# Four chained convolution layers: the second convolution's five shifted products become one, on columns skewed by row

## The reference: what is computed

```
x = x + newton_schulz_inverse(_gn(x), 5 iterations)          # layer 0, one 128x128 matrix per channel
x = x + quantised_conv3x3(_gn(x), weight_int8, scale, bias)   # layer 1
x = x + conv5x5(_gn(x), filter_w[..., :, None] * eye(5))      # layer 2
x = x + circular_conv3x3(_gn(x), weight)                      # layer 3, written with FFTs
```

## Time and profile before

| | |
|---|---|
| three runs | 4611.87, 4616.66, 4623.76 us |
| profiled execution, its own time | 4624.59 us |
| its span | 4622.8 us |
| first stage | up to about 2562 us |
| second stage | the rest, to 4622.8 us |
| TensorE matmul busy | 4399.1 us, 95% of the span |
| VectorE, ScalarE, GpSimd busy | 83%, 49%, 56% |
| mean granted TensorE clock | 0.986 |

### The profile page before, as it was taken

How to read it: one execution, slowest core, us unless ns; L and a number is a source line. 1 busy time by engine, 2 the same in 40 slices (tenths; PEclk the granted TensorE clock), 3 DMA queues, 4 the chain that set the end, 5 groups by cost and what they waited for, 6 DMA issues and landing times. The chain is left out here.

```text
span 4622.8 us, 79863 instructions
## 1 busy us (share of the span) xinstructions
PE 4399.1 (95%) x24265; PEld 3045.4 (66%) x24265; DVE 3833.0 (83%) x8224; ACT 2251.8 (49%) x4551; POOL 2610.2 (56%) x2957
## 2 busy tenths in 40 slices
PE   7999999999999999999999599999999999999998
PEld 6888888888888888888888244444444444444443
DVE  7988898889888988988896687787787778778774
ACT  4766776777677766777776122222222222222221
POOL 7888888888888888888887122222222222222221
PEclk9999999999999999999999799999999999999999
DMA  1111111111111111211111365555556555555554
GB/s 59 61 48 56 56 56 56 56 56 56 56 56 56 56 56 47 63 49 56 56 56 37 84 137 130 130 134 137 125 132 139 127 130 136 132 128 134 137 127 85
DMA packets 333591, 403.08 MB, mean 87 GB/s; under 512 B 23088, under 2 KB 286032, under 8 KB 316880
## 3 DMA queue, kind: packets, MB, share of 16 engines
q1 hardware_dynamic: 284112, 269.46, 18.2%
q10 hardware_dynamic: 49152, 129.59, 16.8%
HBM read 135.22 MB, written 134.22 MB: 58 GB/s over the span
## 5 line engine op out<-in xcount | busy, mean ns | idle before, releaser
L288 POOL TENSOR_TENSOR M<-two,YX 128x256 f32<-128x256 f32 x2560 | 1827.0, 741 | 402.6 <-ACT YX L363 373.4
L758 PE MATMUL bank<-YX,M 128*128 128x256 f32 x8192 | 1948.5, 386 | 40.1 <-issue 40.1
L1147 PE MATMUL bank<-xn,wt 128*128 128x512 f16 (+1 forms) x6912 | 1660.2, 381 | 25.6 <-DVE xn L1003 17.9
L758 PEld LDWEIGHTS bank<-YX,M 128*128 128x128 f32 x8192 | 1504.1, 192 | 227.3 <-issue 44.5
L363 ACT ACTIVATE YX<-bank 128x512 f32<-128x512 f32 x2048 | 1227.5, 599 | 690.8 <-PE bank L758 684.8
L920 POOL TENSOR_TENSOR xn<-F,xn 128x2048 f16<-128x2048 f32 x128 | 487.8, 3811 | 1577.6 <-ACT xn L957 1577.6
L1147 PEld LDWEIGHTS bank<-xn,wt 128*128 128x128 f16 (+1 forms) x6912 | 672.9, 100 | 810.5 <-issue 18.8
L1021 DVE SCALAR_TENSOR_TENSOR x<-bank,wu,x 128x512 f32<-128x512 f32 x512 | 382.2, 746 | 294.7 <-PE bank L1154 283.8
L1154 PE MATMUL bank<-xh,wth 96*128 96x512 f16 (+1 forms) x1792 | 515.4, 380 | 15.3 <-DMA xh<-xn 15.3
L957 ACT ACTIVATE xn<-F 128x2048 f16<-128x2048 f32 x128 | 244.7, 1912 | 475.1 <-DVE F L1077 475.1
L410 DVE BATCH_NORM_STATS2 st<-X 128x6 f32<-128x256 f32 x1024 | 367.8, 410 | 9.6 <-DMA X<-in_x 9.6
(11 more groups left out here) (107 smaller groups left out, 3580.6 us busy)
## 6 DMA issues: line engine op xcount, KB each, us to landing
xh<-xn ACTq DMA_DIRECT2D x768, 131.8 KB, 4.3
X<-in_x SPq DMA_DIRECT2D x64, 1024.0 KB, 4.8
x_scratch<-X SPq DMA_DIRECT2D x64, 1024.0 KB, 5.7
x<-x_scratch SPq DMA_DIRECT2D x64, 1024.0 KB, 6.1
out<-x SPq DMA_DIRECT2D x64, 1024.0 KB, 3.8
xh<-xn ACTq DMA_DIRECT2D x384, 65.9 KB, 2.4
wf<-in_w SPq DMA_DIRECT2D x2, 192.0 KB, 8.5
wf<-in_w SPq DMA_DIRECT2D x1, 320.0 KB, 8.5
```

The costliest lines, as they stand in the source:

```text
L288: nc.gpsimd.tensor_tensor(M[odd][:, at, :], two[:, :].unsqueeze(1).broadcast_to([H, 2, H]), YX[odd][:, at, 0:H], ALU.subtract).then_inc(ma ...
L758: ins = nc.tensor.matmul(banks[u % A_RING][:, 2 * H * m:2 * H * (m + 1)], M[odd][:, 2 * p + m, :], YX[odd][:, 2 * p + m, :], start=True, s ...
L1147: nc.tensor.matmul(bank, wt[l][:, a, k, :], v, start=(k == a == b == 0), stop=False)
```

## The change

The diagonal filter is put on the diagonal of the data. Eight DMAs for an image copy the two f16 halves (`xn2`, now one tile for all images) to a skewed tile `xd`, in which row r of a block lies r columns further left. An output and the five inputs that it reads then stand in the same column, so that one band matrix, the sum of the five, does what five shifted matmuls did. The product comes out skewed too, and over 5 chunks of 423 columns. ScalarE copies it out of PSUM to `yd` (`diagonal_out`), eight more DMAs shift it back to `y` (`unskew`), and GpSimd adds it to x (`third_x`, four instructions), which VectorE did before.

What moves with it:

- The halo of layer 2 takes 4 DMAs of 32 partitions out of `xd`, and two matmuls a chunk in place of three. Matmuls of layer 2 for an image: 5 chunks of 3 + 2, 25 in all, of 423 columns, in place of 72 of 512.
- Image s-1 is in layer 2 in step s as before, but layer 3 now works on image s-3. The steps run to s = 66.
- SyncE's queue now carries, in each step: skew, halos of layer 2, load, unskew, halos of layer 1, store. ScalarE keeps the halo DMAs of layer 3.
- TensorE's order in a step is: layer 1, chunks 0 and 1 of layer 3, the five chunks of layer 2, chunks 2 and 3 of layer 3.
- The first of the three quantising instructions goes from VectorE to ScalarE.
- In the first stage GpSimd zeroes 28,608 columns of tiles in place of 23,760, and the end of the stage prepares the summed weights.

Line numbers of the changed kernel are its own. The diff, cut to the second stage's core:

```diff
+                    def skew(n, odd):
+
+                        stand(sp, normed[2], n + 1, w_loaded, 16 * 15)
+                        for r in range(RB):
+                            rows = slice(C * r, C * r + C)
+                            sp.dma_start(xd[odd][rows, :, LEAD + PW - r:LEAD + PW - r + NJ * PW],
+                                         xn2[rows, :, PW:PW + NJ * PW]).then_inc(skewed[odd], 16)
+
+                    def halos2(n, turn, odd):
+
+                        stand(sp, skewed[odd], 16 * RB * (turn + 1), w_loaded, 16 * 15)
+                        for part in range(2):
+                            for k, (row, at) in enumerate(((RB - 2, UP), (0, DOWN))):
+                                to = 2 * C * (2 * part + k)
+                                sp.dma_start(xh2[odd][to:to + 2 * C, :],
+                                             xd[odd][C * row:C * row + 2 * C, part,
+                                                     at:at + DIAG * DW]).then_inc(halo[2][odd], 16)
+
+                    def unskew(n):
+
+                        stand(sp, evac[2], DIAG * (n + 1), w_loaded, 16 * 15)
+                        for r in range(RB):
...
+                            sp.dma_start(y[rows, :, :],
+                                         yd[rows, at:at + NJ * PW].rearrange("p (j w) -> p j w", w=PW)[:, :, 0:H]).then_inc(unskewed, 16)
...
+                    def step(s, h, slot):
...
+                        if there(s - 1):
+                            skew(s - 1, 1 - odd)
+                            halos2(s - 1, turns(hb, sb_), 1 - odd)
                         if there(s + 2):
+                            load(s + 2, odd)
+                        if there(s - 1):
+                            unskew(s - 1)
+                        if there(s + 1):
+                            halos1(s + 1, 1 - odd)
+                        if there(s - 3):
+                            store(s - 3, place(h, slot, 3)[1])
...
+                    def third_x(n, slot):
+
+                        pool.wait_ge(unskewed, 16 * RB * (n + 1))
+                        for u in range(BPI):
+                            at = slice(4 * u, 4 * u + 4)
+                            nc.gpsimd.tensor_tensor(xs[slot][:, at, :], xs[slot][:, at, :], y[:, at, :],
+                                                    ALU.add).then_inc(x3_new, 1)
...
+                        if there(s - 2):
+                            third_x(s - 2, place(h, slot, 2)[1])
+                            lower(3, s - 2, odd)
                         if there(s):
                             lower(2, s, odd)
...
+                    def step(s, h, slot):
+                        odd = slot % 2
+                        if there(s + 1):
+                            first(s + 1, turns(*place(h, slot, -1)), 1 - odd)
+                        if there(s - 2):
+                            root(3, s - 2)
+                        if there(s - 1):
+                            for u in (0, 1):
+                                diagonal_out(s - 1, u)
+                        if there(s - 2):
+                            upper(3, s - 2, odd)
+                        if there(s - 1):
+                            for u in (2, 3, 4):
+                                diagonal_out(s - 1, u)
+                        if there(s):
+                            root(2, s)
...
+                            upper(2, s, odd)
                         if there(s - 2):
                             wrap(s - 2, odd)
+                            halos3(s - 2, odd)
...
+                        if last:
+                            last_out(s - 3, third, 0)
+                        if old:
+                            normalise(3, s - 2, second)
+                        if now:
+                            deviations(2, s)
+                        if last:
+                            last_out(s - 3, third, 1)
+                        if now:
+                            variance(2, s)
+                        if there(s + 1):
+                            quantise(s + 1, 1 - slot % 2)
+                        if now:
+                            normalise(2, s, slot)
...
+                    def conv2(s, odd, turn, u):
+
+                        bank = chunk_bank(2, u)[:, 0:DW]
+                        at = DOUT + DW * u
+                        if u == 0:
+                            pe.wait_ge(skewed[odd], 16 * RB * (turn + 1))
+                        bank_free(s, 2, u)
+                        for a, b in PRODUCTS:
+                            nc.tensor.matmul(bank, wt2[:, a, :], xd[odd][:, b, at:at + DW], start=a == b == 0, stop=False)
+                        if u == 0:
+                            pe.wait_ge(halo[2][odd], 16 * 4 * (turn + 1))
+                        nc.tensor.matmul(bank, wth2[:, :], xh2[odd][:, DW * u:DW * u + DW], start=False, stop=False)
+                        nc.tensor.matmul(bank, wth2l[:, :], xh2[odd][0:4 * C, DW * u:DW * u + DW], start=False,
+                                         stop=True).then_inc(conv_ps[2], 1)
...
+                        for u in range(DIAG):
+                            if there(s - 1):
+                                conv2(s, 1 - odd, turn2, u)
+                            if now and u == 1:
+                                mean(2, s)
+                            if now and u == 4:
+                                var(2, s)
```

504 lines of the change are left out of this document (287 added, 217 removed).

## The result

The changed kernel took 5359.8 us (median of 4 runs, 5348.0 to 5370.5); the kernel before took 4616.6 in the same rounds. The ratio is 1.161, with a 95% interval of 1.158 to 1.164: 16% slower, where 4% was forecast (4810, range 4590 to 5120). The direction was right, and the time lies outside the range.

The account below looks back on a forecast made before the run. TensorE was taken to bound the kernel before. For the changed one, 2562.0 + 4.7 + 64 x 34.0 + 73.4, plus 1.8 around the span, gave 4818 us profiled, 7.9 less unprofiled: 4810, range 4590 to 5120.

Parts of the forecast that it names:

- Chain A: Closed chain from normed[2] of one image to the next, through skew, halos, layer 2 and quantising; 34.0 us an image.
- SyncE itself ... the queue waits, but is not full: SyncE's queue: 28 DMAs at about 0.65 us are 18 us an image, so it waits but isn't full.
- step 6, the collision: Layer 3's halos, ahead of the skew on the same 16 DMA engines, leave 2.2 us to wait for.
- Period 34: Sign in the loop: one line's starts lie 34 us apart, not 31.2.
- TensorE busy 55 to 65% at a clock under 1.00: Sign in the last stage, with TensorE waiting for the halos of layer 2 and for `var`.
- First skew DMA to first halo matmul about 13.5: Sign in the loop: about 13.5 us from the first skew DMA to layer 2's first halo matmul.
- Quantising some 4.5 us: Sign on VectorE: a quantising instruction takes some 4.5 us in place of 1.23, waiting for GpSimd; cost 3.2 us.
- DMA share above 0.8: Sign on the DMA engines: their busy share is above 0.8.
- the first rival: Skew and halos at 113 GB/s give 5117 us, or layer 2 at half clock on TensorE gives 5066; chance 0.2.
- Memsets and weights: At the start, 4,848 more memset columns on GpSimd cost 4.1 us and the summed weights some 0.6.
- Filling and draining: Last stage outside its 64 image periods: 73.4 us, with 10 us estimated for one more step to drain.
- the faster rival: GpSimd and VectorE don't hold each other up, transfers come near 240 GB/s: loop 29 us, 4490 us; chance 0.18.

Follow-up runs that it names:

- e1: Changed kernel with layer 1's six halo DMAs issued on ScalarE's queue in place of SyncE's; 5286.5 us.
- e3: Changed kernel with 56 unused matmuls an image added ahead of layer 1, layer 2 and its halos to keep TensorE busy; 5296.5 us.
- e13: Changed kernel with the shift back copying each partition as one run of 8432 B in place of 16 runs of 512 B; 5050.0 us.
- e14: Changed kernel with the edits of e11, e13 and e3 together; 5098.7 us.
- e15: Changed kernel with layer 3's halos carrying only the high half, in the same six issues; 5184.9 us.
- e17: Changed kernel with the edits of e11 and e13 together; 5065.2 us.
- e18: e17 with layer 3's halos on SyncE behind layer 2's, and its chunks and halves behind layer 2's; 4854.9 us.
- e9: Changed kernel with all 16 issues of skew and shift back kept, each carrying one partition in place of 16; 4825.1 us.
- e11: Changed kernel with the store issued one step later, behind layer 2's halos, and six result buffers in place of four; 5183.0 us.
- e4: Changed kernel without the 16 DMAs of skew and shift back; 4833.0 us.
- e6: Changed kernel without the eight skew DMAs, the shift back kept; 4880.5 us.
- e7: Changed kernel with all four chunks of layer 3 behind layer 2 on TensorE and their results behind normalise(2) on VectorE; 5401.5 us.
- e8: Changed kernel with the edits of e7 and e1 together; 5456.6 us.

## Why the prediction was wrong

Chain A is the loop, as forecast, but two of its links were priced too low. Each row has the four links in us, their sum, and TensorE's granted clock over layer 2's matmuls; the rows of runs are means over the 26 to 34 images that lie wholly between 3500 and 4700 us.

| | quantising to normed[2] | to the skew landed | to the first halo matmul | layer 2, `var`, to the next quantising | sum | clock in layer 2 |
|---|---|---|---|---|---|---|
| forecast | 10.6 + 3.2 | 8.3 + 2.2 | 5.1 | 4.6 | 34.0 | |
| the image shown | 12.0 | 16.4 | 4.3 | 9.5 | 42.2 | 0.57 |
| changed kernel | 11.2 | 18.9 | 4.3 | 8.4 | 42.8 | 0.64 |
| e1 | 12.9 | 16.3 | 6.3 | 5.7 | 41.2 | 1.00 |
| e3 | 12.9 | 16.4 | 6.2 | 5.7 | 41.2 | 1.00 |
| e13 | 12.9 | 14.3 | 4.3 | 5.7 | 37.2 | 1.00 |
| e14 | 12.8 | 13.5 | 6.3 | 5.7 | 38.3 | 1.00 |
| e15 | 11.1 | 15.4 | 4.3 | 8.6 | 39.4 | 0.62 |
| e17 | 11.4 | 13.6 | 4.4 | 8.2 | 37.6 | 0.66 |
| e18 | 10.6 | 10.2 | 4.9 | 8.5 | 34.2 | 0.62 |

**The step that failed: "SyncE itself ... the queue waits, but is not full", and with it step 6, the collision.** From normed[2] to the landed skew 8.3 + 2.2 = 10.5 us were forecast, and 18.9 measured, 8.4 us more; the whole period is 8.8 longer than forecast. I counted issues, and asked of the queue whether it is busy, not what its transfers leave undone when the skew comes. The skew stands behind the shift back, layer 1's halos and the store. The shift back begins only with layer 2's result, and the others are issued behind it. From 4022.5 to 4035.2 the engines are at 0.96 almost only with the first two: 1.39 of the 1.59 MB that move are of SyncE's queue. Layer 3's halos are issued 2.7 us ahead of normed[2] (forecast 2.5), but by its end only 0.20 of their 0.79 MB have moved. From 4035.2 to the landed skew at 4050.6 the engines work 13.3 of the 15.4 us: 4.9 on the rest of these halos, 8.5 on SyncE's queue, that is the store and the skew. e9 shows that it is the transfers and not the issues, e15 prices the halos, e11 the store's place, e13 the backlog, and e18, with the halos and the store moved behind the skew, has 10.2, near the forecast 10.5.

**The second: layer 2 at the lower clock.** 4.0 us had been worked out and put into a rival; the measured link is 3.8 over the forecast (4.9 in the image shown). Its clock of 0.57 there follows a stretch in which TensorE did 0.75 us in 4.4. That belonged into the sum: layer 2 runs behind this wait in nearly every image. What it costs shows in the links of e1, e3 and e13, where layer 2 ran at a clock of 1.00: 5.7 us in place of 8.4. Of these 2.7 us the period keeps only about 1.0. When layer 2 ends sooner, the quantising starts sooner beside GpSimd's instruction, and its wait grows by 1.7 us (11.2 to 12.9). The other two links were 2.6 and 0.8 us shorter than forecast, which hid part of the two errors.

**Unseen: loop H.** Layer 3's chunks 0 and 1 stand ahead of layer 2 on TensorE, and so their halos are in front of `var` of layer 2. It is 34.4 us without the shifts (e4). In e1 and e3 it is 41.3, but with 6.1 us of moved issues and 3.7 us of unused matmuls that these edits put on it; without them it would be some 35 to 38, an estimate. It holds where the first halo matmul comes 6.2 or 6.3 us after the skew in place of 4.3, because TensorE is still at layer 3: in e1, e3, e9 and e14, and by their chains of waits in e4 and e6. In the changed kernel it doesn't: TensorE waited for layer 3's halos 8.1 us in 28 images, and e7, which opens H, gained nothing. So e1 and e3 gave only 1.5 us because each edit paid on one loop what it saved on the other. Why e7 and e8 are slower than the changed kernel isn't shown by a run of its own; their links differ in the skew (19.4 and 19.8) and in layer 2 (9.0 and 9.2).

**Step by step.** Period 34: 42.7. TensorE busy 55 to 65% at a clock under 1.00: 60% at 0.76 from 3500 to 4700 us, right. First skew DMA to first halo matmul about 13.5: 19.7 in the image shown. Quantising some 4.5 us: its median is 1.46 in the changed kernel, since GpSimd has begun earlier; 3.42 where layer 2 runs at full clock (e4, e13), and 1.23 once GpSimd was moved (e18), so the wait is real and its 3.2 were 2.2. DMA share above 0.8: 0.77 over the loop, since the longer period thins it. The transfers' rate: the skew at 1.08 MB in 7.1 us of engine time is 152 GB/s, not far from 168; the shift back 122. The estimate from the Trainium skill, SBUF — State Buffer, "Door 1: The DMA port swizzle", of 109 for 16 partitions is under both. Both are above the first rival's 113 too, so that rate was not it. That its time (5117) was the nearest is luck. Its other half, the clock (5066), was a real part of the gap, and the smaller one. Memsets and weights: 3.6 for 4.7. Filling and draining: 60 for 73. One sum was slightly off: chain A of the faster rival comes to 34.0 - 3.2 - 2.8 = 28.0, not 28.5; nothing hangs on it.
